# First attention: score products on 64 of the 128 stack rows

## The chip, the cores and the metric

The kernel runs on one core of one Trainium2 chip. The metric is the device time of one execution in microseconds (us). The core has five engines that run side by side, each through its own list of instructions in order: PE (matrix products), DVE (vector), ACT (scalar functions), POOL and SP (here only transfers). They wait for each other through semaphores. PE loads a stationary operand (a weight load, PEld in the profile) and then streams the moving operand past it.

## The reference, cut to what matters

Six stages follow each other on 16 sequences of 256 tokens with 128 features: an expert layer, the first attention, the expert layer again, a zone layer, a second attention, the zone layer again. Only the first attention is touched:

```
q = x @ Wq + bq ; k = x @ Wk + bk ; v = x @ Wv + bv    # 16 query heads, 4 key groups, 8 features a head
scores = einsum('bghnd,bhsd->bghns', q, k)
attn = softmax(scores / 8 ** 0.5, axis=-1)
out = einsum('bghns,bhsd->bghnd', attn, v)
return out @ Wo + bo
```

The four query heads of a key group share its keys and values.

## The kernel before, in words

A head has only 8 features, so the kernel stacks things over the 128 rows (partitions). Each of the 4 key groups has a block of 32 rows: three copies of 8 rows for a rounded value, a remainder and a product of the two, and two rows in which the query's maximum is subtracted. `QS0` is the query stack of a sequence: columns are 4 heads (j, one of each group) times 256 queries. `KS0` is the key stack, kept four times: copy g holds zeros in all rows but the 32 of group g. A product over all 128 rows with copy g so gives the scores of group g alone.

Every sequence (b) passes through 16 slots (m). In each slot PE makes one `scores` product (queries on rows of the output, 2 groups times 256 keys in 512 columns, banks 0 and 1 in turn) for the sequence ahead, and one `scores_t` product (the transposed scores, keys on rows, two heads times 256 queries, banks 2 and 3) for the present one. DVE takes the maximum over keys of each `scores` result (`smax`), ACT the exponential of each `scores_t` result (`exps`). `scores` may run one slot ahead of `smax` and `scores_t` one ahead of `exps`, since each has two banks.

Between the slots' products PE does the rest of the work, in the order that `step` of `a0_pe` writes out: `key_value` in slot 0, `values` of four groups in slots 1, 5, 9 and 13, `queries` in 1 and 3, the transposes `turn` in 4 and 12, `back` in 7 and `maxima` in 13, `project_out` in 10. The `values` products have an output of 32 rows and are placed on four column quarters of the array; everything else is over the whole array, 128 by 128. In the first two steps, when there is no `scores_t` yet, `keep_busy` puts a small product behind each `scores`.

DVE's `step` has `smax` in each slot and, between them, `vals`, `key_stacks` (makes the copies of `KS0`), `normalise`, `stacks`, `maxima`, `add` and `shift`. `key_value` and `scores_t` of a sequence wait for the two halves of `shift`, which put the maxima into the query stack.

The lines that the change touches are L738 (`scores`), L746 (`scores_t`), L759 (`values`), L907 (`key_stacks`), L922 (`smax`) and L947 (`normalise`). Other lines that the rows show: L705 and L707 `key_value`, L716 `queries`, L725 `maxima`, L768 `turn`, L774 `back`, L780 `project_out`, L170 `keep_busy`, L853 `exps`, L864 the copy that `project_out` waits for, L838 and L846 the queries' copies on ACT, L897 `vals`, L938 `shift`. L1394 and L1395 belong to another stage: two products into the same output, one over 128 rows and one over 33 (placed on 64), eight times in turn:

```
pe.matmul(o, R.ukt[:, h * KAP:(h + 1) * KAP], R.uqt[:, h * P:(h + 1) * P], start=True, stop=False)
last = pe.matmul(o, R.qrp[0:DC1 + 1, h * KAP:(h + 1) * KAP], R.spread[0:DC1 + 1, :], start=False, stop=True)
```

L1405, behind them, is eight products over 128 rows.

Of the kernel before, what the change touches and what calls it, by code (L numbers as in the profile page):

```python
# [86 lines left out]
def program(nc, a, out, stages):  # L87
    ctx = ExitStack()
    with ctx:
# [9 lines left out]
        def bank(k, n=1):  # L99
            return PS[:, k:k + n, :].rearrange("p b n -> p (b n)")  # L100
# [40 lines left out]
        def small(n):  # L141
            sm_at[0] += n
            assert sm_at[0] <= 4352
            return SM[:, sm_at[0] - n:sm_at[0]]
# [12 lines left out]
        small(-sm_at[0] % 8)  # L157
        small(NH1 * P)
        BSB = nc.alloc_sbuf_tensor_at("BSB", [P, NH1 * P], F32R, offset=sm_base + 4 * (sm_at[0] - NH1 * P))
        WKAP2, B1K2, POWER = small(P), small(1), small(1)  # L160
        cg = small(2 * H)
        cb = small(H)
        rev, ident, ones = T.rev, T.ident, T.ones
# [512 lines left out]
        QX0 = XN.rearrange("p u t h -> p (u t h)")  # L676
        QS0 = [XHI[:, u * 1024:(u + 1) * 1024] for u in range(3)]
        QH0 = XHI[:, 3072:4096]
        KS0 = [XLO[:, u * 1024:(u + 1) * 1024].rearrange("p (g k) -> p g k", g=4) for u in range(3)]
        KH0 = XLO[:, 3072:3328]  # L680
        NS0 = NH0

# [9 lines left out]
                g.tensor_tensor(xs, xs, T.bo.unsqueeze(1).to_broadcast([P, TPC, H]), ALU.add).then_inc(S.xb, 1)  # L692

        LEAD = 4

        def a0_pe(n):
            S = ST[n]
# [29 lines left out]
                last.then_inc(S.mt, 1)  # L727

            def scores(b, m):
                k, j, gp = m // 8, m // 2 % 4, m % 2  # L730
                if m == 0:
                    pe.wait_ge(S.ks, b + 1)
                    if b == 0:
                        pe.wait_ge(S.xt, NC)
                if m in (0, 4):
                    pe.wait_ge(S.qs, 2 * b + m // 4 + 1)
                wait(pe, S.smax, NS0 * b + m - 1)
                pe.matmul(bank(m % 2), QS0[b % 3][:, j * SEQ + k * P:j * SEQ + (k + 1) * P], KS0[b % 3][:, 2 * gp:2 * gp + 2, :],  # L738
                          start=True, stop=True).then_inc(S.s_pe, 1)

            def scores_t(b, m):
                if m < 2:
                    pe.wait_ge(S.qs2, 2 * b + m + 1)
                wait(pe, S.exp, NS0 * b + m - 1)
                g, k, jp = m // 4, m // 2 % 2, m % 2
                pe.matmul(bank(2 + m % 2), KS0[b % 3][:, g, k * P:(k + 1) * P], QS0[b % 3][:, jp * 512:(jp + 1) * 512],  # L746
                          start=True, stop=True).then_inc(S.st_pe, 1)

            def values(b, g):
                pe.wait_ge(S.exp, NS0 * b + 4 * g + 4)  # L750
                if g == 0:
                    pe.wait_ge(S.v, b + 1)
                    wait(pe, S.ao, 2 * b - 1)
                if g == 2:
                    wait(pe, S.x_new, b)
                o = bank(6 + g // 2)
                for k in range(2):
                    for j in range(4):
                        last = pe.matmul(o[32 * j:32 * j + 32, g % 2 * SEQ:(g % 2 + 1) * SEQ], VA3[:, b % 3, k, g, :],  # L759
                                         PT[:, g % 2, k, j, :], start=(k == 0), stop=(k == 1), skip_group_check=True)  # L760
                last.then_inc(S.av, 1)

# [124 lines left out]
        def a0_dve(n):  # L887
            S = ST[n]
            v = nc.vector
            norm_dve(n)  # L890
            rchain, mchain, kchain = Chain(v, S.r_chain), Chain(v, S.m_chain), Chain(v, S.k_chain)

            def vals(b):
                v.wait_ge(S.kx, b + 1)
                wait(v, S.av, 4 * (b - 2))
                for k in range(2):
                    last = v.tensor_tensor(VA3[:, b % 3, k, :, 0:HD0],  # L897
                                           bank(4)[:, SEQ + k * 32:SEQ + (k + 1) * 32].rearrange("p (g d) -> p g d", g=4),
                                           T.bvb.rearrange("p (g d) -> p g d", g=4), ALU.add)
                last.then_inc(S.v, 1)  # L900

            def key_stacks(b, part):
                if part == 0:
                    wait(v, S.st_pe, NS0 * (b - 2))
                    kchain.link(v.scalar_tensor_tensor(KSF0, KH0.bitcast(F32), T.masks[:, 1:2], KX0, ALU.mult, ALU.add))
                for g in (2 * part, 2 * part + 1):
                    last = v.tensor_scalar(KS0[b % 3][:, g, :], KSF0, T.masks[:, 2 + g:3 + g], None, ALU.mult)  # L907
                if part:
                    last.then_inc(S.ks, 1)

            def stacks(b, half):
                v.wait_ge(S.qh, 2 * b + half + 1)
                wait(v, S.st_pe, NS0 * (b - 2))
                at = slice(half * 512, (half + 1) * 512)
                v.scalar_tensor_tensor(QS0[b % 3][:, at], QH0[:, at].bitcast(F32), T.masks[:, 0:1], QX0[:, at],
                                       ALU.mult, ALU.add).then_inc(S.qs, 1)

            def smax(b, m):
                if m == 0:
                    wait(v, S.mm, b)  # L920
                v.wait_ge(S.s_pe, NS0 * b + m + 1)
                v.tensor_reduce(MX[:, 2 * m:2 * m + 2], bank(m % 2).rearrange("p (h k) -> p h k", h=2), AX.X, ALU.max)\  # L922
                    .then_inc(S.smax, 1)

            def maxima(b):
                v.wait_ge(S.smax, NS0 * (b + 1))
                wait(v, S.mt, b)
                if b == 0:
                    v.wait_ge(S.zero, 1)
                mchain.link(v.tensor_copy(MH, MX))  # L930
                mm = MM0.rearrange("p (n c) -> p n c", c=32)
                v.tensor_copy(mm[:, :, 24], MH.bitcast(F32))
                v.tensor_tensor(mm[:, :, 25], MX, MH.bitcast(F32), ALU.subtract).then_inc(S.mm, 1)

            def shift(b, half):
                v.wait_ge(S.mt, b + 1)
                at = slice(half * 512, (half + 1) * 512)
                v.tensor_tensor(QS0[b % 3][:, at], QS0[b % 3][:, at].bitcast(F32), bank(4 + half), ALU.add).then_inc(S.qs2, 1)  # L938

            def normalise(b, half):  # L940
                v.wait_ge(S.ot, 2 * b + half + 1)
                wait(v, S.aot_pe, b)
                t = bank(6 + half).rearrange("p (x i) -> p x i", i=32)
                rd = RD[:, half * 16:(half + 1) * 16]
                rchain.link(v.reciprocal(rd, t[:, :, HD0]))
                for k in range(2):
                    last = v.tensor_tensor(AO0[:, k * P + half * 64:k * P + half * 64 + 64].rearrange("p (x i) -> p x i", i=HD0),  # L947
                                           t[:, k * 8:(k + 1) * 8, 0:HD0],
                                           rd[:, k * 8:(k + 1) * 8].unsqueeze(2).to_broadcast([P, 8, HD0]), ALU.mult)
                last.then_inc(S.ao, 1)  # L950

            def add(b):
                v.wait_ge(S.out, b + 1)
                v.wait_ge(S.xb, b // 2 + 1)
                xs = X[:, b * TPB:(b + 1) * TPB, :]
                v.tensor_tensor(xs, xs, bank(7)[:, SEQ:2 * SEQ].rearrange("p (t h) -> p t h", t=TPB), ALU.add).then_inc(S.x_new, 1)
                v.wait_ge(S.x_new, b + 1)
                for t in range(TPB):
                    last = v.bn_stats(STAT[:, b * TPB + t, :], X[:, b * TPB + t, :])
                last.then_inc(S.st_new, 1)  # L960

            def step(i):
                now, next_, far, done = (0 <= i + d < NB for d in (0, 1, 2, -1))
                for m in range(NS0):
                    b, s = divmod(NS0 * (i + 1) + LEAD + m, NS0)
                    if 0 <= b < NB:
                        smax(b, s)
                    if m == 2 and far:
                        vals(i + 2)
                    if m in (3, 4) and far:  # L970
                        key_stacks(i + 2, m - 3)
                    if m == 5 and done:
                        normalise(i - 1, 1)
                    if m in (8, 9) and far:
                        stacks(i + 2, m - 8)
                    if m == 11 and next_:
                        maxima(i + 1)
                    if m == 12 and done:
                        add(i - 1)
                    if m == 13 and now:  # L980
                        normalise(i, 0)
                    if m in (14, 15) and next_:
                        shift(i + 1, m - 14)

            for i in range(-2, NB + 1):
                step(i)
# [1262 lines left out]
```

## Time and profile before

| what | value |
|---|---|
| median of 3 runs | 1557.27 us (1553.46 to 1557.97) |
| the profiled execution | 1556.08 us, its span 1554.1 us |
| mean granted clock of PE in it | 0.969 of full speed |
| PE busy | 1468.7 us, 94% of the span |
| DVE busy | 1098.9 us, 71% |
| ACT busy | 956.7 us, 62% |
| POOL busy | 581.1 us, 37% |
| first attention, from the first `scores` to the last `add` | about 320 to 658 us |

The span runs from the first to the last instruction, and the time also has the 2 us around it. A PE record covers a product from its start until its result is out, so records of products that follow closely overlap, and PE's busy share says little about room. What tells is the distance between starts, or the chain of waits, where a product counts for the time from the end of the one before it to its own. PE handles float32 operands in two passes, so each such product has two records (x4 is two products); the score products are float32r and have one.

### The profile page before, as it was taken

The page shows a single profiled execution, that of the slowest core. Times are in us where ns is not written, and L with a number is a line of the kernel's source. Part 1 is how long each engine was busy: PE and PEld are TensorE (multiplying, and loading weights), DVE is VectorE, ACT ScalarE, POOL GpSimd, SP SyncE. Part 2 cuts the span into 40 slices and gives each one's busy share as a digit, 9 for nine tenths or more (in the row PEclk, how much of TensorE's full clock was granted, in tenths as well). Part 3 has the DMA queues.
Part 4 walks back from the last instruction along what each step waited for, and adds up shares of the span by engine and source line. Part 5 has one row for each costly group of instructions (what it writes and reads, how often), then busy time and mean ns, then how long its engine had stood idle before and what let it go on. Part 6 is the DMA issues. An engine that isn't in the chain of part 4 may idle for free.

```text
span 1554.1 us, 27551 instructions
## 1 busy us (share of the span) xinstructions
PE 1468.7 (94%) x9774; PEld 1199.3 (77%) x9774; DVE 1098.9 (71%) x2377; ACT 956.7 (62%) x1710; POOL 581.1 (37%) x551
## 2 busy tenths in 40 slices
PE   6999999889999999899999999899988999989998
PEld 6888888765555556488888888799977777768998
DVE  3766766778888888466766764477768888866765
ACT  6455555446666666655555555577736666668886
POOL 4466666500000000006666664377720111126664
PEclk7999999999999999969999996799999999999999
DMA  6000000000000000000000004000000000000000
GB/s 172 1 1 1 1 1 1 1 1 1 1 1 1 1 1 1 1 1 1 1 1 1 0 1 165 1 2 1 2 1 1 1 2 2 1 2 1 15 15 28
DMA packets 13318, 16.85 MB, mean 11 GB/s; under 512 B 768, under 2 KB 10496, under 8 KB 12928
## 3 DMA queue, kind: packets, MB, share of 16 engines
q1 hardware_dynamic: 13184, 15.11, 3.1%
q8 instruction: 78, 1.28, 0.3%
q14 instruction: 56, 0.46, 0.1%
HBM read 13.01 MB, written 2.10 MB: 10 GB/s over the span
## 4 chain that ended last, share of the span: by engine, by line
PE 81%; ACT 7%; DVE 7%; issue 4%; DMA 1%; POOL 0%; SPq 0%; DVEq 0%; POOLq 0%; ACTq 0%
PE PS L602 19%; PE PS L630 10%; PE PS L1736 9%; PE PS L1749 8%; PE PS L759 3%; PE PS L738 3%; PE PS L746 3%; PE PS L170 2%; ACT AR L853 2%; PE PS L716 2%; PE PS L1106 2%; PE PS L1110 2%; PE PS L1081 2%; PE PS L424 1%; PE PS L1063 1%
## 5 line engine op out<-in xcount | busy, mean ns | idle before, releaser
L540 POOL TENSOR_TENSOR RR<-AR,RR 128x512 fp32r<-128x512 f32 x150 | 193.8, 1292 | 520.9 <-ACT RR L563 520.9
L577 ACT ACTIVATE AR<-PS 128x512 f32<-128x512 f32 x224 | 134.0, 598 | 197.3 <-PE PS L602 196.1
L519 DVE TENSOR_TENSOR AR<-AR,PS 128x512 f32<-128x512 f32 x224 | 153.6, 686 | 132.4 <-PE PS L602 132.4
L853 ACT ACTIVATE AR<-PS 128x512 f32<-128x512 f32 x256 | 149.5, 599 | 98.2 <-PE PS L746 96.8
L922 DVE TENSOR_REDUCE AR<-PS 128x2 f32<-128x512 f32 x256 | 173.3, 686 | 47.3 <-PE PS L738 46.2
L602 PE MATMUL PS<-XHI,WG 128*128 128x512 f32 x448 | 175.8, 392 | 0.0
L602 PE MATMUL PS<-XHI,WU 128*128 128x512 f32 x448 | 174.6, 390 | 0.2
L523 DVE TENSOR_TENSOR AR<-AR,PS 128x512 f32<-128x512 f32 x224 | 153.8, 687 | 8.0 <-POOL RR L540 0.4
L1736 PE MATMUL PS<-XHI,SL 128*128 128x256 f32 x576 | 133.8, 288 | 2.4 <-DVE XTR L1902 1.4
L1736 PE MATMUL PS<-XLO,SL 128*128 128x256 f32 x576 | 133.0, 286 | 1.5 <-DVE XTR L1902 1.3
L1826 ACT ACTIVATE PS<-PS 128x1024 f32<-128x1024 f32 x96 | 96.8, 1009 | 55.0 <-PE PS L1736 54.6
L2013 POOL CAST SL<-ZW 128x1024 fp32r x96 | 100.4, 1045 | 79.6 <-PE PS L1749 78.7
L738 PE MATMUL PS<-XLO,XHI 128*128 128x512 f32 x256 | 122.5, 479 | 5.9 <-DVE AR L922 4.8
L630 PE MATMUL PS<-RR,WD 128*128 128x512 f32 x450 | 126.4, 390 | 1.5 <-POOL RR L540 1.5
L1749 PE MATMUL PS<-XTR,SL 128*128 128x256 f32 x640 | 123.8, 283 | 0.3 <-DVE XTR L1902 0.3
L1902 DVE SCALAR_TENSOR_TENSOR XTR<-PS,AR,RR 128x512 fp32r<-128x512 f32 x128 | 90.1, 745 | 48.0 <-ACT RR L1836 48.0
L540 POOL TENSOR_TENSOR H<-AR,H 128x512 fp32r<-128x512 f32 x74 | 95.6, 1292 | 58.6 <-ACT H L563 58.5
L1287 DVE TENSOR_REDUCE AR<-PS 128x2 f32<-128x512 f32 x128 | 87.2, 683 | 36.5 <-PE PS L1081 36.3
L746 PE MATMUL PS<-XHI,XLO 128*128 128x512 f32 x256 | 105.0, 413 | 1.9 <-ACT AR L853 1.2
L2011 POOL CAST SL<-ZW 128x1024 fp32r x96 | 99.7, 1039 | 11.6 <-DVE IDX L1665 8.9
L1749 PE MATMUL PS<-RR,SL 128*128 128x256 f32 x512 | 102.7, 283 | 0.0
L1736 PEld LDWEIGHTS PS<-XHI,SL 128*128 128x128 f32 x576 | 99.6, 191 | 3.3 <-issue 1.6
(299 smaller groups left out, 3476.8 us busy)
## 6 DMA issues: line engine op xcount, KB each, us to landing
X<-in_x SPq DMA_DIRECT2D x4, 512.0 KB, 6.4
RAWZ<-in_zone_up SPq DMA_DIRECT2D x8, 256.0 KB, 5.1
RAWZ<-in_zone_down SPq DMA_DIRECT2D x8, 256.0 KB, 5.6
out_x<-X SPq DMA_DIRECT2D x4, 512.0 KB, 3.2
AR<-in_w SPq DMA_DIRECT2D x1, 1792.0 KB, 11.7
XT<-in_w SPq DMA_DIRECT2D x1, 1608.0 KB, 8.7
XT<-in_sel SPq DMA_DIRECT2D x1, 896.0 KB, 7.3
SM<-in_small SPq DMA_DIRECT2D x1, 857.5 KB, 6.9
```

Source lines behind the costliest of these rows:

```text
L519: v.tensor_tensor(PRD[:, m % 2, :], SIL[:, m % 2, :], bank(2 + m % 2), ALU.mult).then_inc(S.prod, 1)
L523: v.tensor_tensor(GAT[:, m % 2, :], PRD[:, m % 2, :], bank(4 + m // SHARED), ALU.mult).then_inc(S.gated, 1)
L540: g.tensor_tensor(HL[k % 3], GAT[:, m % 2, :], HH[k % 3].bitcast(F32), ALU.subtract).then_inc(S.h_lo, 1)
L577: act.activation(SIL[:, m % 2, :], bank(m % 2), ACT.Silu).then_inc(S.silu, 1)
L602: last = pe.matmul(out, w[i][:, m * P:(m + 1) * P], x[:, bass.ds(c * 512, 512)], start=(j == 0), stop=(j == 2))
L630: last = pe.matmul(bank(6), WD[i][:, m, :], h[k % 3], start=(m == 0 and j == 0), stop=(m == MT0 - 1 and j == 2))
L738: pe.matmul(bank(m % 2), QS0[b % 3][:, j * SEQ + k * P:j * SEQ + (k + 1) * P], KS0[b % 3][:, 2 * gp:2 * gp + 2, :], start=True, stop=True) ...
L746: pe.matmul(bank(2 + m % 2), KS0[b % 3][:, g, k * P:(k + 1) * P], QS0[b % 3][:, jp * 512:(jp + 1) * 512], start=True, stop=True).then_inc( ...
L853: act.activation(PT[:, g % 2, k, 2 * jp:2 * jp + 2, :], bank(2 + m % 2).rearrange("p (j q) -> p j q", j=2), ACT.Exp, scale=SC0).then_inc(S ...
L922: v.tensor_reduce(MX[:, 2 * m:2 * m + 2], bank(m % 2).rearrange("p (h k) -> p h k", h=2), AX.X, ALU.max)\
L1736: last = pe.matmul(o, SL[:, k, 0, i, m * P:(m + 1) * P], x[:, b * SEQ:(b + 1) * SEQ], start=(j == 0), stop=(j == 2))
L1749: last = pe.matmul(bank(4 + b % 2)[:, 0:SEQ], SL[:, k, 1, i, m * P:(m + 1) * P], h[z % 3][:, at], start=(k == 0 and m == 0 and j == 0), st ...
```

## The change

The four masked key copies become two. Copy o (0 or 1) keeps groups o and o + 2, so the 64 upper rows (groups 0 and 1) of it hold one group, and so do the 64 lower rows (groups 2 and 3). A score product now takes one half of the rows, h: `scores` streams both copies' rows of that half and gets groups 2h and 2h + 1; `scores_t` takes copy g % 2 in half g // 2. `ORDER` lets the groups of `scores_t` (and so `values`, `exps`, `normalise`) come as 0, 2, 1, 3, and the heads and halves of `scores` are numbered so that in each slot its half is the opposite one to that of `scores_t`. The number of products, their columns, banks and semaphores stay as they are. In the built program the score products are placed on 64 by 128 of the array, at row 0 or row 64, where they were on 128 by 128. `key_stacks` has two instructions for four, one more makes `ODD` once, and `normalise` writes through other strides.

```diff
-        KS0 = [XLO[:, u * 1024:(u + 1) * 1024].rearrange("p (g k) -> p g k", g=4) for u in range(3)]
+        KS0 = [XLO[:, u * 512:(u + 1) * 512].rearrange("p (o k) -> p o k", o=2) for u in range(3)]
@@ a0_pe
+        ORDER = (0, 2, 1, 3)
+        def half_rows(h):
+            return slice(h * 64, h * 64 + 64)
             def scores(b, m):
-                k, j, gp = m // 8, m // 2 % 4, m % 2
+                k, h, j = m // 8, m // 4 % 2, m % 4
...
-                if m in (0, 4):
-                    pe.wait_ge(S.qs, 2 * b + m // 4 + 1)
+                if m in (0, 2):
+                    pe.wait_ge(S.qs, 2 * b + m // 2 + 1)
                 wait(pe, S.smax, NS0 * b + m - 1)
-                pe.matmul(bank(m % 2), QS0[b % 3][:, j * SEQ + k * P:j * SEQ + (k + 1) * P], KS0[b % 3][:, 2 * gp:2 * gp + 2, :],
-                          start=True, stop=True).then_inc(S.s_pe, 1)
+                pe.matmul(bank(m % 2), QS0[b % 3][half_rows(h), j * SEQ + k * P:j * SEQ + (k + 1) * P],
+                          KS0[b % 3][half_rows(h), :, :], start=True, stop=True).then_inc(S.s_pe, 1)
             def scores_t(b, m):
...
-                g, k, jp = m // 4, m // 2 % 2, m % 2
-                pe.matmul(bank(2 + m % 2), KS0[b % 3][:, g, k * P:(k + 1) * P], QS0[b % 3][:, jp * 512:(jp + 1) * 512],
+                g, k, jp = ORDER[m // 4], m // 2 % 2, m % 2
+                rows = half_rows(g // 2)
+                pe.matmul(bank(2 + m % 2), KS0[b % 3][rows, g % 2, k * P:(k + 1) * P], QS0[b % 3][rows, jp * 512:(jp + 1) * 512],
                           start=True, stop=True).then_inc(S.st_pe, 1)
@@ values
-                        last = pe.matmul(o[32 * j:32 * j + 32, g % 2 * SEQ:(g % 2 + 1) * SEQ], VA3[:, b % 3, k, g, :],
+                        last = pe.matmul(o[32 * j:32 * j + 32, g % 2 * SEQ:(g % 2 + 1) * SEQ], VA3[:, b % 3, k, ORDER[g], :],
@@ a0_dve
+            kchain.link(v.tensor_tensor(ODD, T.masks[:, 2:4], T.masks[:, 4:6], ALU.add))
@@ key_stacks
-                for g in (2 * part, 2 * part + 1):
-                    last = v.tensor_scalar(KS0[b % 3][:, g, :], KSF0, T.masks[:, 2 + g:3 + g], None, ALU.mult)
+                ins = v.tensor_scalar(KS0[b % 3][:, part, :], KSF0, ODD[:, part:part + 1], None, ALU.mult)
```

PE's order in a middle step, slots 2 to 5, before the change (L738 and L746 the two score products, L716 `queries`, L768 `turn`, L759 `values`):

```order
L738 MATMUL PS<-XLO,XHI 128x512
L746 MATMUL PS<-XHI,XLO 128x512
L716 MATMUL PS<-XT,SM 128x256 x2
L738 MATMUL PS<-XLO,XHI 128x512
L746 MATMUL PS<-XHI,XLO 128x512
L768 MATMUL PS<-SM,AR 128x128 x4
L738 MATMUL PS<-XLO,XHI 128x512
L746 MATMUL PS<-XHI,XLO 128x512
L759 MATMUL PS<-AR,SM 32x256 x8
```

And now (L743 and L752 the score products, L721 `queries`, L774 `turn`, L765 `values`):

```order
L743 MATMUL PS<-XLO,XHI 128x512
L752 MATMUL PS<-XHI,XLO 128x512
L721 MATMUL PS<-XT,SM 128x256 x2
L743 MATMUL PS<-XLO,XHI 128x512
L752 MATMUL PS<-XHI,XLO 128x512
L774 MATMUL PS<-SM,AR 128x128 x4
L743 MATMUL PS<-XLO,XHI 128x512
L752 MATMUL PS<-XHI,XLO 128x512
L765 MATMUL PS<-AR,SM 32x256 x8
```

Nothing moved on PE; what is new is that a pair L743, L752 sits on halves of the array's rows between neighbours that take all of its rows.

DVE's order in the same slots before (L922 `smax`, L897 `vals`, L905 and L907 `key_stacks`, L945 and L947 `normalise`):

```order
L897 TENSOR_TENSOR SM<-PS,SM 128x4x8 x2
L922 TENSOR_REDUCE AR<-PS 128x2
L905 SCALAR_TENSOR_TENSOR AR<-XLO,SM,AR 128x256
L907 TENSOR_SCALAR XLO<-AR,SM 128x256 x2
L922 TENSOR_REDUCE AR<-PS 128x2
L907 TENSOR_SCALAR XLO<-AR,SM 128x256 x2
L922 TENSOR_REDUCE AR<-PS 128x2
L945 RECIPROCAL AR<-PS 128x16
L947 TENSOR_TENSOR AR<-PS,AR 128x64 x2
```

And now (L929 `smax`, L904 `vals`, L912 and L913 `key_stacks`, L952 and L956 `normalise`):

```order
L904 TENSOR_TENSOR SM<-PS,SM 128x4x8 x2
L929 TENSOR_REDUCE AR<-PS 128x2
L912 SCALAR_TENSOR_TENSOR AR<-XLO,SM,AR 128x256
L913 TENSOR_SCALAR XLO<-AR,SM 128x256
L929 TENSOR_REDUCE AR<-PS 128x2
L913 TENSOR_SCALAR XLO<-AR,SM 128x256
L929 TENSOR_REDUCE AR<-PS 128x2
L952 RECIPROCAL AR<-PS 128x16
L956 TENSOR_TENSOR AR<-PS,AR 128x2x32 x2
```

The two pairs of mask multiplications have become single ones, in the same places.

## Rows read from the trace of the kernel before

**Rows 1.** The page: granted clock in 40 slices, and the chain by engine.

```profile
PEclk7999999999999999969999996799999999999999
PE 81%; ACT 7%; DVE 7%; issue 4%; DMA 1%; POOL 0%; SPq 0%; DVEq 0%; POOLq 0%; ACTq 0%
```

**Rows 2.** Windows: stretch, length, busy time of PE, PEld, DVE, ACT, POOL, granted clock.

```profile
500.00:600.00 100.00, 92.99 (x655) 58.41 (x655) 82.27 (x190) 65.94 (x133) 0.00 (x0) 1.00 0.00 1
499.92:520.36 20.44, 19.00 (x132) 11.86 (x132) 16.89 (x40) 13.42 (x27) 0.00 (x0) 1.00 0.00 1
```

**Rows 3.** Groups by line in 338 to 651 us: busy, mean ns, idle before.

```profile
L922 DVE TENSOR_REDUCE AR<-PS 128x2 f32<-128x512 f32 x237 | 160.8, 686 | 45.8 <-PE PS L738 45.0
L853 ACT ACTIVATE AR<-PS 128x512 f32<-128x512 f32 x254 | 148.4, 599 | 97.3 <-PE PS L746 95.9
L907 DVE TENSOR_SCALAR XLO<-AR,SM 128x256 fp32r<-128x256 f32 x56 | 17.1, 349 | 0.5
```

**Rows 4.** The chain in 499.9 to 520.4 us: start, us, what.

```profile
501.16 0.67 PE PS L705 x2
...
502.20 0.31 PE PS L738
502.51 0.24 PE PS L746
502.75 1.00 PE PS L759 x16
503.75 1.06 PE PS L716 x4
504.81 0.24 PE PS L738
...
506.11 1.10 PE PS L716 x4
507.21 0.23 PE PS L738
...
509.58 0.43 PE PS L738
...
511.73 0.52 ACT XHI L846
...
514.77 0.23 PE PS L738
```

**Rows 5.** Weight loads, then products, of slot 4: timeline, 507.8 to 508.6 us.

```profile
507.84 0.19 PEld L738 LDWEIGHTS PS<-XLO,XHI 128*128 128x128 f32 x1
507.95 0.19 PEld L746 LDWEIGHTS PS<-XHI,XLO 128*128 128x128 f32 x1
...
508.19 0.40 PE L746 MATMUL PS<-XHI,XLO 128*128 128x512 f32 x1
```

**Rows 6.** Timeline of slot 8: its `scores_t`, its exponential on ACT.

```profile
511.13 0.40 PE L746 MATMUL PS<-XHI,XLO 128*128 128x512 f32 x1
...
512.12 0.61 ACT L853 ACTIVATE AR<-PS 128x512 f32<-128x512 f32 x1
```

**Rows 7.** The chain in 319 to 360 us, where the attention fills.

```profile
321.53 0.22 PE PS L170 x2
...
324.43 0.87 PE PS L716 x4
...
329.21 2.48 DVE AR L922 x4
```

**Rows 8.** The chain at L1394 and L1395, which take turns, and PE's timeline behind.

```profile
974.28 0.62 PE PS L1394 x2
974.90 0.62 PE PS L1395 x2
...
983.52 3.73 PE L1405 MATMUL PS<-RRF,XT 128*128 128x128 f32 x16
```

**Rows 9.** Windows of that stretch, PE alone: busy, granted clock.

```profile
972.90:983.00 10.10, 10.10 (x35) 0.50 0.00 0
```

More of the change, by code:

```diff
@@ L159, in program @@
         BSB = nc.alloc_sbuf_tensor_at("BSB", [P, NH1 * P], F32R, offset=sm_base + 4 * (sm_at[0] - NH1 * P))
-        WKAP2, B1K2, POWER = small(P), small(1), small(1)
+        WKAP2, B1K2, POWER, ODD = small(P), small(1), small(1), small(2)
         cg = small(2 * H)
@@ L905, in key_stacks @@
                     kchain.link(v.scalar_tensor_tensor(KSF0, KH0.bitcast(F32), T.masks[:, 1:2], KX0, ALU.mult, ALU.add))
-                for g in (2 * part, 2 * part + 1):
-                    last = v.tensor_scalar(KS0[b % 3][:, g, :], KSF0, T.masks[:, 2 + g:3 + g], None, ALU.mult)
+                ins = v.tensor_scalar(KS0[b % 3][:, part, :], KSF0, ODD[:, part:part + 1], None, ALU.mult)
                 if part:
-                    last.then_inc(S.ks, 1)
+                    ins.then_inc(S.ks, 1)
             def stacks(b, half):
@@ L921, in smax @@
                 v.wait_ge(S.s_pe, NS0 * b + m + 1)
-                v.tensor_reduce(MX[:, 2 * m:2 * m + 2], bank(m % 2).rearrange("p (h k) -> p h k", h=2), AX.X, ALU.max)\
+                at = m // 8 * 16 + m % 4 * 4 + m // 4 % 2 * 2
+                v.tensor_reduce(MX[:, at:at + 2], bank(m % 2).rearrange("p (h k) -> p h k", h=2), AX.X, ALU.max)\
                     .then_inc(S.smax, 1)
@@ L946, in normalise @@
                 for k in range(2):
-                    last = v.tensor_tensor(AO0[:, k * P + half * 64:k * P + half * 64 + 64].rearrange("p (x i) -> p x i", i=HD0),
-                                           t[:, k * 8:(k + 1) * 8, 0:HD0],
-                                           rd[:, k * 8:(k + 1) * 8].unsqueeze(2).to_broadcast([P, 8, HD0]), ALU.mult)
+                    out_ = AO0[:, k * P:(k + 1) * P].rearrange("p (g j i) -> p g j i", g=4, i=HD0)[:, half:4:2]
+                    sums = rd[:, k * 8:(k + 1) * 8].rearrange("p (g j) -> p g j", g=2).unsqueeze(3)
+                    last = v.tensor_tensor(out_, t[:, k * 8:(k + 1) * 8, 0:HD0].rearrange("p (g j) i -> p g j i", g=2),
+                                           sums.to_broadcast([P, 2, 4, HD0]), ALU.mult)
                 last.then_inc(S.ao, 1)
```

## The prediction

> **What bounds the kernel now.** I read the page first. The chain that ends last lies on PE for 81% of the span, and the granted clock stands at 9 or more in the slices of the first attention (the ninth to the seventeenth) [rows 1]: PE runs there at its upper level, 2.4 GHz. The windows say that 100 us in the middle of this stage hold 82.3 us of DVE and 65.9 us of ACT, and that one sequence takes 20.44 us, with 16.9 us of DVE in it [rows 2]. So no engine is full by its work: DVE has 3.5 us of room in each sequence, ACT has 7. The groups by line say who waits for whom: DVE's `smax` waited 45.0 us for the `scores` product and ACT's `exps` 95.9 us for `scores_t` [rows 3]. PE is what the others wait for.
>
> The chain through one sequence then says where [rows 4]. It goes on PE almost without a break from `key_value` (501.16) to `scores` of slot 2, takes one turn over DVE (`smax`, `vals`), goes on PE again from `queries` (506.11) over slots 4 and 5 to slot 6, then lies on ACT from about 510.3 to 514.0, on PE once more from `project_out` over slot 11 (514.77) to slot 14, and closes over ACT and DVE, which finish almost together. A score product on this path costs 0.23 or 0.24 us.
>
> **What the change removes.** Two mask multiplications a sequence, 349 ns each by their records, about 0.3 us each by their distance: 0.6 us of DVE. They are in slots 3 and 4, where the chain lies on PE, so in the middle of the stage I count nothing for them. If PE were faster than DVE, DVE would be the bound at 16.9 - 0.6 = 16.3 us a sequence; that is far off.
>
> **What it may give on PE.** The two products of a slot now sit on different rows of the array and write different banks. Before, they stand one behind the other, 0.23 us apart. How much sooner can the second start? Its weights come 0.11 us behind the first one's (507.84 and 507.95), their load takes 0.19 us, so they are in at 508.14 at the latest, and the product started at 508.19 [rows 5]. From the starts of the loads the second product could lie 0.11 behind the first instead of 0.23. I take 0.10 us for a pair. The bounds are 0 (the two don't overlap) and 0.23 (the second costs nothing). That parts of the array can work together this trace shows for column quarters: the 8 products of `values`, 256 float32 columns each, take 1.00 us, while 2 such products of `queries` over the whole array take 0.87 [rows 4, 7]. For row halves no row shows it.
>
> The second product counts on the path in slots 1, 4, 5, 6, 11, 12 and 13: 7 x 0.10 = 0.70. Slots 11 and 12 follow each other directly, so there the third product may start early as well; I add 0.13. Together 0.83 us a sequence. In slots 2, 3, 14 and 15 the path is over DVE and in 7 to 10 over ACT: nothing.
>
> **What it costs on PE.** The products around the pairs still take all rows. The trace has three places where PE goes from one shape to another. Behind `values` (column quarters) the products of `queries` took 1.06 us, and 0.87 where nothing of another shape stands ahead: 0.19. Behind `values` again, a `scores` product took 0.43 instead of 0.24: 0.19 [rows 4, 7]. Into `values`: four rounds at the 0.217 of a pass of `queries` are 0.87, and it takes 1.00: 0.13. Are these costs of column quarters alone? L1394 and L1395 say no: they alternate between 128 and 64 rows, 0.62 us for each two passes of 128 columns, while L1405 has its 16 passes in 3.73 us, 0.23 each or less, so 0.46 for two. A change between 128 and 64 rows there costs 0.16 us [rows 8]. That stretch has a granted clock of 0.50 [rows 9], yet the figure agrees with those at full clock. I take 0.19 for leaving a full-array piece to a pair and 0.13 for the way back.
>
> The Trainium skill says the same in "TensorEngine Tiling (Array Packing)", section Key Properties: a change of tiling mode, unlike a change of tile, drains the array. The trace agrees, by the 0.62 us of the alternating products. The same page's section Theoretical Speedup gives up to 2x for a contraction of at most 64, and by that figure alone each pair would cost one product's 0.23 us less, on the eight places above 1.84 us a sequence; that is the upper bound I already have from the rows, and it leaves out what the drains cost.
>
> Now the places. Before, only the four `values` groups change shape. After, each neighbour of a pair does. New on the path, leaving to a pair: behind `key_value` (slot 0), `queries` (1), `queries` (3), `turn` (4), `project_out` (10), `turn` (12): 6 x 0.19 = 1.14. New on the path, away from a pair: into `turn` (4), `turn` (12), `maxima` (13): 3 x 0.13 = 0.39. Covered: into `key_value`, the second `queries` and `project_out`, because PE waits there anyway (for `shift`, `vals` and the copy on ACT), and both sides of `back` in slot 7, because ACT holds the path from slot 6 to 10 (the `scores_t` of slot 8 ended at 511.53, 0.6 us before ACT came to it at 512.12 [rows 6]). The changes of shape at `values` are paid in both kernels. Sum 1.53 us. If the cover at slot 7 were gone, 0.32 more.
>
> Net: 1.53 - 0.83 = 0.70 us a sequence, later. Nobody's wait is shortened by it: `smax` and `exps`, which wait for PE now, wait longer. Over the 15 sequences whose steps are full: 10.5 us.
>
> **The fill**, 320 to 338 us. Here each `scores` is followed by a `keep_busy` product over the whole array, 0.22 us [rows 7]. A slot becomes 0.23 + 0.22 + 0.19 + 0.13 = 0.77 us on PE, against 0.62 us that DVE needs (2.48 for 4). For some 10 slots that were DVE's that is 1.5 us, the six first slots, PE's already, can lose up to 0.32 each. Against it, DVE is the path here, and half of the mask multiplications go, 0.6 us. Between -0.6 and 3; I take 2.
>
> **The rest**: the waits for the query stack in slot 2 instead of 4 are met three slots earlier; `ODD` is one small operation; other strides in `normalise` move the same 64 columns. Nothing. Sum: 10.5 + 2 = 12.5 us on 1556.1 of the profiled execution, 1568.6. That execution is 1.2 us under the median, so 1569 for the changed kernel's median.
>
> **The rivals.**
> (a) No overlap at all: the row halves run one after the other and the shape changes are paid. 1.53 x 15 = 23, and 3 for the fill: 1582 us. Against it: the four column quarters do overlap. 0.12.
> (b) The two balance: pairs overlap by 0.19 to 0.23 on the eight places (1.5 to 1.84) against 1.53. From +2 to -4 us: 1553 to 1559, mostly no change. It needs the weight load of the second to lie wholly ahead of the first product, which the 0.11 between the loads speaks against. 0.16.
> (c) On the other side: the way between halves and whole array costs nothing, because a 64-row product leaves the array sooner or the next load is let past it. Then only the overlap is left, 0.83 to 1.84 us a sequence, 12 to 28 us: 1544 to 1529. It decides from the point where a shape change costs under 0.83 / 9 = 0.09 us. Rows 8 speak against it with 0.16, but for float32 products with short weight loads; the overlapped pair might also take work out of the places that DVE and ACT hold now, by freeing banks sooner. 0.21.
> (d) The clock. In 972.9 to 983 PE shows 10.10 of 10.10 us busy, with shapes changing all the time, and is granted 0.50, which is 1.2 GHz [rows 9]. If the first attention fell to that level, its PE pieces of the chain, some 13 us a sequence, would grow by up to as much: over 100 us. Before that stretch PE had waited, and here it never does for long. 0.03.
>
> **How the numbers follow.** The forecast, slower by 5 to 20 us, has 0.48. Slower in all: 0.48 + 0.12 + 0.03 = 0.63. Within 0.3% (4.7 us, about what a measurement can tell from no change): most of (b), 0.15. Faster: (c) and the rest of (b), 0.22. The range reaches up over (a), 1583, and down over (b) into (c), 1546; the forecast alone would be 1562 to 1577.
>
> **What would show it.** In the changed trace the distance from the start of L743 to that of L752 in one slot should be about 0.13 us where nothing else holds them, instead of 0.23. Behind `turn` and `queries` the first `scores` should count 0.42 on the chain instead of 0.23, with its weight load not begun before the full-array work has ended. The stage should take about 21.1 us a sequence instead of 20.44, the waits of `smax` and `exps` for PE should grow, the granted clock stay at 1.00, and everything outside the stage keep its length. The prediction is wrong if weight loads of the halves are still let in ahead (then c), if pairs start within a few tens of ns of each other (then b or c), or if the DVE work that went was late in a way that the chain doesn't show.

## The result, and the profile after

The changed kernel takes 1583.41 us (median of 5, 1569.27 to 1606.39), the kernel before 1557.16 (1552.94 to 1557.97): the ratio is 1.0156, 95% interval 1.0103 to 1.021. In a second series (e8) it took 1593.47 us (median of 6, 1575.92 to 1608.15) against 1557.2, ratio 1.0236 (1.0199 to 1.0274). Ratios leave out executions more than 1.5% above a kernel's fastest. The spread, 37 and 32 us where the kernel before has 5, is the first thing to explain. In the profiled execution the last `add` comes 13.3 us later than before and the span is 13.2 us longer, so nothing outside the stage changed its length.

The page of the changed kernel, granted clock in 40 slices and the chain by engine:

```profile
PEclk7999999989999999969999997799999999999999
PE 78%; DVE 10%; ACT 6%; issue 5%; DMA 1%; POOL 0%; SPq 0%; DVEq 0%; POOLq 0%; ACTq 0%
```

Two things differ from [rows 1]: PE gave 3 points of the chain away, and DVE took them; and in the ninth slice, where the stage begins, the clock is no longer at 9. The windows of the changed kernel's stage, PE alone (stretch, length, busy, granted clock):

```profile
320.00:340.00 20.00, 19.57 (x80) 1.00 0.00 1
340.00:370.00 30.00, 25.83 (x141) 0.77 0.00 1
370.00:610.00 240.00, 206.50 (x1550) 1.00 0.00 1
610.00:640.00 30.00, 25.90 (x171) 0.89 0.00 1
```

The kernel before had 1.00 all through 320 to 650 us. Here the clock falls for a time. From 340 us on PE is 86% busy in each of the stretches, in the low ones as in the high one (in the first one, the fill, 98%). This is the profiled execution, the fastest of the five: the others have mean clocks over the span of 0.953, 0.953, 0.951 and 0.935, this one 0.961. A line through the 11 executions of both series has 13 us for each 0.01 of mean clock and leaves no one further off than 3.0 us; carried on to 0.968, where the kernel before stands and none of the 11 does, it gives 1563. So by this estimate some 6 us of the change are work and waits, and the rest, 20 us and more at the median, is the clock.

The chain through a sequence at full clock (start, us, what), changed kernel:

```profile
511.48 0.43 PE PS L743
511.91 0.00 PE PS L752
511.91 1.00 PE PS L765 x16
512.91 1.06 PE PS L721 x4
513.97 0.44 PE PS L743
...
516.57 0.42 PE PS L743
516.99 0.00 PE PS L752
517.00 0.59 PE PS L774 x4
```

Against [rows 4]: the first product of a pair counts 0.42 to 0.44 where it counted 0.23, 0.24 or, in slot 1, 0.31; `turn` counts 0.59 instead of 0.44; and the second product of a pair counts nothing. `turn` before:

```profile
507.68 0.44 PE PS L768 x4
```

In the fill, `keep_busy` behind a `scores` product counts 0.42 where it counted 0.22 [rows 7]:

```profile
320.23 0.42 PE PS L170 x2
```

The timeline of slot 1 shows why the second product counts nothing:

```profile
511.41 0.18 PEld L743 LDWEIGHTS PS<-XLO,XHI 64*128 64x128 f32 x1
511.41 0.50 PE L743 MATMUL PS<-XLO,XHI 64*128 64x512 f32 x1
511.41 0.18 PEld L752 LDWEIGHTS PS<-XHI,XLO 64*128 64x128 f32 x1
511.41 0.50 PE L752 MATMUL PS<-XHI,XLO 64*128 64x512 f32 x1
```

Both weight loads and both products have one start. The Trainium skill, "TensorE: Matmul & The Clock Gate", section Packing small matmuls, gives some 4 ns between tiles on different rows; the trace agrees, within its 10 ns. Of the 229 pairs that the timeline lists singly, 198 have starts within 10 ns of each other. A sequence takes 20.57 to 20.60 us from `add` to `add`, in all 11 intervals between the falls of the clock, where it took 20.42 to 20.44. In 338 to 651 us `smax` waited 62.9 us for `scores` and `exps` 104.8 us for `scores_t`, where they had waited 45.0 and 95.9 [rows 3].

### The profile page after: what moved, and what is told of

Its sections match the earlier page's. It is cut to its first block, busy times and chain, and to the rows that moved or that the text cites. A ratio compares the mean times of both kernels' runs of the same rounds, so it can differ in the third digit from the quotient of the medians.

```text
span 1567.3 us, 27521 instructions
## 1 busy us (share of the span) xinstructions
PE 1464.2 (93%) x9774; PEld 1171.1 (75%) x9774; DVE 1093.3 (70%) x2346; ACT 956.2 (61%) x1710; POOL 581.1 (37%) x551
## 3 DMA queue, kind: packets, MB, share of 16 engines
q8 instruction: 78, 1.28, 0.3%
## 4 chain that ended last, share of the span: by engine, by line
PE 78%; DVE 10%; ACT 6%; issue 5%; DMA 1%; POOL 0%; SPq 0%; DVEq 0%; POOLq 0%; ACTq 0%
PE PS L602 19%; PE PS L630 10%; PE PS L1744 9%; PE PS L1757 8%; PE PS L743 3%; PE PS L170 3%; PE PS L765 3%; PE PS L721 2%; DVE AR L929 2%; PE PS L1114 2%; PE PS L1118 2%; PE PS L1089 2%; PE PS L1071 1%; PE PS L424 1%; ACT AR L859 1%
## 5 line engine op out<-in xcount | busy, mean ns | idle before, releaser
L929 DVE TENSOR_REDUCE AR<-PS 128x2 f32<-128x512 f32 x256 | 173.8, 687 | 67.8 <-PE PS L743 66.1
L743 PE MATMUL PS<-XLO,XHI 64*128 64x512 f32 x256 | 114.5, 484 | 14.4 <-DVE AR L929 12.3
L752 PE MATMUL PS<-XHI,XLO 64*128 64x512 f32 x256 | 113.4, 484 | 2.5 <-ACT AR L859 1.0
```

Of the source, the lines that this page charges most:

```text
L743: pe.matmul(bank(m % 2), QS0[b % 3][half_rows(h), j * SEQ + k * P:j * SEQ + (k + 1) * P], KS0[b % 3][half_rows(h), :, :], start=True, stop ...
L752: pe.matmul(bank(2 + m % 2), KS0[b % 3][rows, g % 2, k * P:(k + 1) * P], QS0[b % 3][rows, jp * 512:(jp + 1) * 512], start=True, stop=True) ...
L929: v.tensor_reduce(MX[:, at:at + 2], bank(m % 2).rearrange("p (h k) -> p h k", h=2), AX.X, ALU.max)\
```

## The experiments

The mean clocks of each kernel's executions are given with the times, since they carry the answer; the kernel before has 0.966 to 0.973 beside them. Sequences are measured from `add` to `add` in the profiled execution.

**e1: both products of a slot on the same half.**

```diff
-                k, h, j = m // 8, m // 4 % 2, m % 4
+                k, h, j = m // 8, 1 - m // 4 % 2, m % 4
-                at = m // 8 * 16 + m % 4 * 4 + m // 4 % 2 * 2
+                at = m // 8 * 16 + m % 4 * 4 + (1 - m // 4 % 2) * 2
```

> The changed kernel, with the half of the scores product flipped, so that both products of a slot take the same 64 rows (the sums stay right, MX is filled in the flipped order). Theory A (opposite halves let the second product of a slot start with the first, and each change between halves and the whole array costs about 0.2 us): the pair is back at 0.23 us from start to start, a sequence goes from 20.59 to between 22.2 and 22.4 us (7 or 8 places of 0.23), 25 us in all: about 1593 us where the clock stays up. Theory B (the two products start together because of their records alone, nothing is gained by opposite halves): 20.6 us a sequence and no change of the whole. On the clock: if the granted clock falls because the overlapping pairs leave the array too little to do, this kernel has fewer such stretches than the changed one (mean clock 0.965 or more in each run, spread under 5 us); if it falls because of the shape changes, it has as many.

Measured: 1639.37 us (1628.87 to 1664.54), ratio 1.05 (1.047 to 1.053), mean clocks 0.907 to 0.932. The chain at full clock, then the windows, PE alone:

```profile
416.36 0.23 PE PS L752
...
417.61 0.24 PE PS L752
```

```profile
320.00:400.00 80.00, 78.25 (x266) 0.59 0.00 1
400.00:430.00 30.00, 28.32 (x193) 1.00 0.00 1
430.00:510.00 80.00, 76.97 (x303) 0.57 0.00 1
```

The second product is back at 0.23 us, and a sequence at full clock takes 21.72 us: the opposite halves are worth 1.13 us, less than expected, as much as the whole 0.23 at five places. Against 20.44 of before, the shapes alone cost 1.28 us. Theory A's mechanism held and its time did not: the clock fell more than in the changed kernel, to 0.57 over 80 us. In the 30 us ahead of that fall PE was at 1.00 and 94% busy, more than the 86% of the changed kernel. So it is not that the overlap leaves PE too little time at work.

**e2: the removed work of DVE put back**, two more mask multiplications into unused columns.

```diff
+                v.tensor_scalar(XLO[:, 1536 + 256 * part:1792 + 256 * part], KSF0, ODD[:, part:part + 1], None, ALU.mult)
```

> The changed kernel with two mask multiplications a sequence added on DVE, in the places of those removed, into unused columns. Theory A (DVE's saved 0.6 us a sequence lies off the path in the full steps): 20.6 us a sequence, as in the changed kernel, and at most 0.6 us more in the fill. Theory B (DVE is close enough to the path that its saved work is what keeps the changed kernel near the old one): 20.9 to 21.2 us a sequence, 5 to 9 us more in all.

Measured: 1582.73 us (1574.06 to 1589.31), mean clocks 0.948 to 0.96, and 20.58 to 20.61 us a sequence at full clock. The halved mask work is worth nothing there, as theory A had it. The time is the changed kernel's.

**e3: the fill's filler on 64 rows.**

```diff
-                        keep_busy(pe, bank(2), 1)
+                        pe.matmul(bank(2)[:, 0:P], ident[0:64, :], ident[0:64, :], start=True, stop=True)
```

> The changed kernel with the filler product of the first two steps of the attention taken over 64 rows too, so that the fill has no shape change between scores and filler. Theory A (the fill lost some 3 us to shape changes, and the clock falls at 340 to 370 us because the drained array of the fill looks idle): the slot of the fill goes from 0.84 to about 0.45 us on PE, the sequence starts 3 us sooner, and no stretch under 1.00 is left before 400 us; median 1560 to 1566. Theory B (the clock falls because products over 64 rows count for less, whatever the changes of shape): the fill is 3 us shorter, but the granted clock falls there as before or more; median 1575 to 1590.

Measured: 1591.93 us (1577.3 to 1595.86), ratio 1.0215 (1.0175 to 1.0256), mean clocks 0.939 to 0.957. Windows, PE alone:

```profile
320.00:350.00 30.00, 27.35 (x102) 0.55 0.00 1
350.00:560.00 210.00, 184.21 (x1172) 0.86 0.00 1
```

Without shape changes between scores and filler the clock fell in the fill all the same, to 0.55, and theory B stands, with a median 2 us above its band: it is not the shape changes between those two. The 3 us that the shorter fill should give can't be read off, since the clock fell within it.

**e4: the transposes moved next to other full-array work** (`turn` to slots 5 and 13, `back` to 9, `normalise` to slot 6 and to slot 0 of the next step). Of its diff, one place:

```diff
-                    if m == 12 and now:
+                    if m == 13 and now:
                         turn(i, 0)
```

> The changed kernel with turn moved from slots 4 and 12 to 5 and 13, ahead of values and maxima, back from 7 to 9, ahead of values, and DVE's normalise from 5 to 6 and from 13 to slot 0 of the next step. That takes away six shape changes a sequence, four of them on the chain, and takes normalise (0.6 us) out of the DVE stretch that closes a sequence. Theory A (shape changes cost 0.13 to 0.2 us each on the path): 19.3 to 19.9 us a sequence, 10 to 19 us less in all than the changed kernel. Theory B (the path has slack enough, DVE and ACT close it): 20.4 to 20.6 us.

Measured: 1600.92 us (1589.76 to 1621.3), ratio 1.0268 (1.0234 to 1.0301), mean clocks 0.929 to 0.951; at full clock 20.90 us a sequence, in the other stretches up to 23.9. Both theories missed. The chain at full clock shows what took the place of the shape changes:

```profile
417.36 0.44 PE PS L743
...
418.43 0.26 DVE AR L952
418.69 0.02 issue
418.71 0.35 DVE AR L956 x2
419.06 0.61 DVE AR L929
```

DVE's `normalise` (L952, L956) now stands between two `smax` that PE waits for. It had been where DVE had room. The edit moved several things at once, so it does not tell what the six shape changes are worth. But with six fewer in a sequence the mean clocks are no higher than the 0.934 to 0.961 of the changed kernel, which speaks against the shape changes as the reason for its falls.

**e5: shape changes alone, in the kernel before**: score products over all rows, with a small 64-row product (its result is written over) ahead of 7 of 16.

```diff
+                if m in (1, 5, 6, 8, 9, 12, 15) or NS0 * b + m < 20:
+                    pe.matmul(bank(m % 2)[:, 0:8], ident[0:64, :], ident[0:64, 0:8], start=True, stop=True)
```

> The kernel before, score products over all 128 rows, with a product of 64 rows and 8 columns put ahead of seven of the 16 scores products of a sequence (those that follow key_value, queries, turn, back, project_out) and ahead of each in the fill: 14 changes of shape more a sequence, about as many as the change brought, and its result is written over at once. Theory A (the clock falls because of the products over half the rows): the granted clock stays at 1.00 from 320 to 650 us in every execution, mean clock 0.966 or more, and a sequence takes 1.3 to 3 us more than 20.44 (a way there and back of 0.33 us or a bit more at 4 to 7 places): 1578 to 1602 us with a spread under 5 us. Theory B (the clock falls because each change of shape drains the array): stretches at 0.50 to 0.9 show up as in the changed kernel, mean clock 0.96 or less, spread over 10 us.

Measured: 1609.56 us (1605.04 to 1611.52), ratio 1.034 (1.0327 to 1.0353), mean clocks 0.963 to 0.971. The small product (L739) and `scores` behind it (L740) on the chain, then the windows, PE alone:

```profile
417.67 0.32 PE PS L739 x2
417.99 0.44 PE PS L740
```

```profile
320.00:370.00 50.00, 46.91 (x275) 1.00 0.00 1
370.00:650.00 280.00, 264.45 (x1724) 0.98 0.00 1
620.00:640.00 20.00, 18.68 (x115) 0.91 0.00 1
```

A sequence takes 23.36 us, inside theory A's 1.3 to 3 us more; the product behind a 64-row one counts 0.43 or 0.44, as expected of a shape change. The time is 8 us above theory A's band, the spread is 6.5 us instead of under 5, and three of the five mean clocks lie under its 0.966. The first `add` alone comes 11.2 us later than before. The clock mostly stays: the profiled execution has three drops in the stage, of about 3 us each (one of them makes the 0.91 above), and each costs 1.5 us. This and e1 are the pair that decides: both have 32 score products a sequence, none overlapped, and 14 shape changes more than the kernel before, both keep PE 94% busy at the upper level, and they differ in the rows of the score products. They come from two series; the kernel before had 0.966 to 0.973 in one and 0.967 to 0.972 in the other. e5 even spreads its work over 23.4 us a sequence instead of 21.7. Over half the rows the clock is 0.57 for 80 us at a time, over all rows 0.98. Theory A holds for the bulk. Whether the short drops of e5 come from its shape changes, as theory B would have it, no run shows.

**e6: eight fillers a sequence over the whole array, in PE's waits.**

```diff
+                    if m in (0, 3) and i > 0:
+                        pe.wait_ge(S.ao, 2 * i - 1)
+                        keep_busy(pe, bank(6), 3)
+                    if m == 15 and now:
+                        pe.wait_ge(S.ao, 2 * i + 1)
+                        keep_busy(pe, bank(6), 2)
```

> The changed kernel with eight filler products a sequence over the whole array (128 columns, into bank 6, which is free then), in the three places where PE waits with nothing to do: ahead of key_value, ahead of the second queries, and behind the last slot. Theory A (half-row products count for less than whole ones, so the full steps stand just at the edge of what keeps the clock up): with 1.7 us more of full work the clock stays at 1.00 in the full steps, a sequence takes 20.6 to 20.9 us, and only the fill may still lose; median 1562 to 1572, spread under 10 us. Theory B (the clock falls because of the changes of shape, or of something that filler work doesn't touch): as many stretches below 1.00 as in the changed kernel, median 1580 or more.

**e7: as e6, and two fillers for one in the fill.**

> As e6, and two filler products in place of one behind each scores product of the fill. Theory A: the fill grows by 0.2 us a slot, 4 us in all, and keeps its clock at 1.00, which by the earlier traces is worth 5 to 15 us; median 1560 to 1568, spread under 6 us, the least of all kernels with half-row products. Theory B: 4 us more than e6 and the same spread.

Measured, e6: 1569.97 us (1566.1 to 1579.49), mean clocks 0.957 to 0.965. Measured, e7: 1569.44 us (1569.11 to 1569.67), ratio 1.0081 (1.0068 to 1.0094), mean clocks 0.966 to 0.969. Windows of e6, then of e7:

```profile
320.00:370.00 50.00, 48.17 (x157) 0.59 0.00 0
370.00:660.00 290.00, 278.95 (x2093) 1.00 0.00 1
```

```profile
320.00:660.00 340.00, 327.18 (x2392) 1.00 0.00 1
```

The median of e6 is where theory A had it, though its spread is 13 us and not under 10; e7 is a microsecond or two above its band. With 1.7 us of useless full-array products a sequence, all full steps of e6 and e7 are at 1.00 and take 20.57 to 20.61 us, and what is left of the spread in e6 is the fill. With two fillers there too it is gone: 37 us have become 0.6. The fillers also raise PE's busy share in the full steps, from 86% to 96%; but e1 fell from 94%, where the kernel before keeps 1.00 at 93% [rows 2], so the share alone doesn't decide it. In e7 the fill pays for it, since the first `add` comes at 383.61 us, 9.7 after that of the kernel before.

**e8: the changed kernel again.**

> The changed kernel as it is, on the same chip as e5 to e7 and against the same runs of before, for the distribution of its time and its clock. Both theories: median 1575 to 1590, mean clocks from 0.935 to 0.962, and the time falls with the mean clock, some 13 us for each 0.01, which would leave it at 1557 to 1562 at the 0.969 of the kernel before. If instead the executions of one clock differ by more than 5 us, something besides the clock spreads them.

Measured: 1593.47 us (1575.92 to 1608.15), mean clocks 0.934 to 0.959, the median 3 us above the band that both theories gave. In the profiled one 340 to 470 us have a granted clock of 0.84, five sequences take 22.1 to 23.7 us, and the next seven 20.57 to 20.61. Finer windows show what a mean of 0.84 is made of:

```profile
388.00:394.00 6.00, 6.00 (x29) 0.50 0.00 0
395.00:411.00 16.00, 13.52 (x100) 1.00 0.00 0
412.00:418.00 6.00, 6.00 (x29) 0.50 0.01 3
```

The clock is at its lower level for some 6 us, once in each of these sequences, and at the upper one in between. Time and clock go together as said at the start.

**e9, e10, e11: is it DVE that closes a sequence at full clock?** In the changed kernel the chain no longer goes over `turn`, `maxima` and `values` from slot 11, but over DVE:

```profile
503.44 0.44 PE PS L743
...
503.89 0.70 DVE AR L929
...
506.43 0.28 DVE STAT L967
506.71 0.59 DVE AR L929
507.30 0.17 DVE AR L952
...
507.49 0.35 DVE AR L956 x2
...
507.86 0.69 DVE AR L929
508.56 0.60 DVE XHI L945
```

e9 is e7 with `bn_stats` moved to slot 1 of the next step and the fill's second filler only where scores run; e10 has the fill's fillers in fours behind each second product; e11 is the kernel before with `bn_stats` moved.

```diff
                     if m == 12 and done:
                         add(i - 1)
+                        if i == NB:
+                            stats(NB - 1)
+                    if m == 1 and 0 <= i - 2 < NB:
+                        stats(i - 2)
```

> e7 with add's two bn_stats moved from slot 12 to slot 1 of the next step, where DVE has nothing to do, and the second filler of the fill only where scores products run. Theory A (at full clock a sequence of the changed kernel is closed by DVE: the chain runs over smax, maxima, add, bn_stats, normalise and shift from slot 11 to 15, which eats what the overlap gives): 0.4 to 0.5 us less a sequence, 20.1 to 20.2, and 1.8 us less in the fill: 1559 to 1563 us. Theory B (PE's shape changes are the bound there): 20.5 to 20.6 us a sequence and 1567 to 1568.

> e9 with the fill's filler products in fours behind each second scores product instead of in twos behind each: half the shape changes of the fill, as much full work. Theory A (a way there and back costs 0.4 us with 10 such places gone, partly covered by DVE's smax): 2 to 4 us less than e9, 1556 to 1560 us, clock kept. Theory B (the fill is held by DVE once PE has less to do, or the clock falls in it): within 1 us of e9 or slower, with a larger spread.

> The kernel before with bn_stats moved in the same way. Theory A (the kernel before is closed by PE in slots 11 to 13, so DVE's work there costs it nothing): 20.44 us a sequence and the same time within 2 us. Theory B (DVE closes the sequence in both kernels): 20.0 us a sequence and 6 us less.

Measured, e9: 1566.72 us (1561.39 to 1570.87), ratio 1.0066 (1.0042 to 1.0089), mean clocks 0.964 to 0.974, 20.57 to 20.61 us a sequence. Measured, e10: 1563.93 us (1560.28 to 1564.9), ratio 1.0047 (1.0028 to 1.0066), mean clocks 0.967 to 0.974. Measured, e11: 1556.95 us (1551.65 to 1557.94), ratio 1.0002 (0.999 to 1.0015). For e9 theory A fell: the sequence did not get shorter. Its chain says why:

```profile
461.03 0.43 PE PS L743
461.46 0.30 PE PS L752 x2
461.76 0.62 PE PS L774 x4
462.38 0.43 PE PS L743
462.81 0.00 PE PS L752
462.81 1.07 PE PS L730 x8
463.89 0.05 issue
463.94 1.07 PE PS L765 x16
```

With DVE's 0.45 us gone the path is PE's, and from `project_out` to the next `scores_t` it still takes 6.5 us: from slot 11 to 15 both engines need about the same time, and neither can be shortened alone. In the kernel before that stretch was PE's, and e11, where nothing changed, agrees. Theory A holds only so far. e10 bears out the price of the fill's shape changes: its first `add` comes at 378.52 after 381.0 of e9, 2.5 us for half of them, and its median is 2.8 us under that of e9, if 4 above theory A's band. It is the best version with half-row products and still 0.5% behind the kernel before. No version found beats that one.

## Why the prediction was right, and where it was not

Slower was right. That the time lies at the upper edge of the range is luck: the forecast itself was 5 to 20 us, 12.5 by its sum, and the medians are 26 and, in the second series, 36 us up. What fills the gap is the clock, rival (d), which had 3%, and the edge at 1583 had been set by rival (a), no overlap, which is the opposite of what the trace shows.

- **Shape changes**, 0.19 behind full-array work and 0.13 back: right. The chain has 0.43 for 0.23 or 0.24 behind it; on the way back it has 0.59 for 0.44 at `turn` and 0.42 for 0.22 at the filler. e1 has them alone, with 1.28 us a sequence against the 1.53 of the sum.
- **Overlap**, 0.10 us a pair: too small. It is the whole 0.23, the upper bound. The step that failed here is the reading that a load 0.11 us behind the first holds the second product back by as much: loads that follow 0.11 apart on the same rows start together on opposite ones. By the prediction's own sign, pairs that start within a few tens of ns, its middle case was wrong. e1 puts the overlap at 1.13 us a sequence, not 0.83. It is less than 8 x 0.23, for 1.13 / 0.23 is five places, since the chain left PE for DVE from slot 11 on.
- **The net of a full step** was therefore +0.15 instead of +0.70 us, near rival (b), where the two balance, though both of its terms came out smaller.
- **The fill**: +2.6 us (`key_value` of the first full step at 341.97 on the chain after 339.37) for the 2 of the sum.
- **Masks on DVE**: nothing in the full steps, right (e2).
- **The clock**: the step that failed, that the granted clock would "stay at 1.00". It was priced as one drop over the whole stage, over 100 us. In the two profiled executions of the changed kernel it came as drops of 3 to 10 us, and their number differs from one execution to the next. The reason it was put aside was that PE had waited ahead of the stretch at 0.50 [rows 9] and here never does for long. But the clock was down there before the products of that stretch began, so the rows could say nothing of what products over fewer rows do to it:

```profile
960.00:972.90 12.90, 11.77 (x58) 0.50 0.00 1
```

Without the clock the change costs some 6 us, and the sum had 12.5. Two errors partly cancel: the full steps were put 8 us too high (10.5 for 15 x 0.15), and the clock, which the sum left out, took 20 us at the median.

What stays open is which property of a half-row product counts for less, what decides in which execution the clock falls, and whether the short drops in e5 come from the shape changes: no run measured the array's activity itself.

## What to carry to other kernels

Here products on opposite halves of the rows overlapped entirely, but each passage between them and full-array work cost 0.15 to 0.2 us on the path, so pairs scattered between other products gave it all back. Count the passages; half-row work in longer runs would have fewer, which no run here tried. Products over half the rows kept the clock up less well than products over all rows, even though masks made half of the latter's rows useless (e1 against e5). Where a kernel's spread grows from 5 to 37 us, look at the mean clock of each execution before anything else, and try filler products in PE's waits.

## What the runs showed of the hardware that was not expected

- Two products of 64 rows on opposite halves, each with 512 float32r columns, start with their weight loads within the same 10 ns (changed kernel); on the same half they are 0.23 us apart (e1).
- With PE 94% busy at 1.00, half-row score products were followed by 80 us at 0.57 (e1); with PE 94% busy and full-row ones the clock was 0.98 over 280 us (e5).
- Eight products of 128 by 128 float32 a sequence, 1.7 us in 20.6, came with a clock of 1.00 over 290 us (e6), in a stage where it had fallen in one execution and not in another, and cost nothing, being in waits: 20.58 to 20.61 us a sequence against 20.57 to 20.60.
